# The last head pair of layer 4: recombined by two small matmuls in place of transfers

## The reference, cut to what matters

```
q = heads(_layernorm(x) @ Wq.T + bq)        # 16 heads of 16 channels
k, v = heads(ctx @ Wk.T + bk), heads(ctx @ Wv.T + bv)
w = softmax(q @ k.T / sqrt(16))             # 256 x 4096 for a head, 4 batches
out = merge(w @ v)                          # 256 tokens x 256 channels
x = x + out @ Wo.T + bo
```

## Time and profile before

| what | value |
|---|---|
| the three runs | 2039.83, 2045.66, 2051.41 us (median 2045.66) |
| the profiled execution | 2051.41 us, span 2051.5 us |
| busy in the span | PE 88%, DVE 74%, ACT 59%, POOL 11% |
| mean granted clock of TensorE | 0.943 of full |
| layer 4, pairs 0 to 31 | up to 1845.4 us in the span |
| its chain behind the last pair | 1845.4 to 1865.0 us |

### The profile page before, as it was taken

How to read it: one execution, slowest core, us unless ns; L and a number is a source line. 1 busy time by engine, 2 the same in 40 slices (tenths; PEclk the granted TensorE clock), 3 DMA queues, 4 the chain that set the end, 5 groups by cost and what they waited for, 6 DMA issues and landing times. The chain is left out here.

```text
span 2051.5 us, 32916 instructions
## 1 busy us (share of the span) xinstructions
PE 1795.8 (88%) x12549; PEld 1222.8 (60%) x12549; DVE 1518.3 (74%) x1768; ACT 1205.8 (59%) x2132; POOL 234.1 (11%) x243
## 2 busy tenths in 40 slices
PE   7989998878888885799998799999999999996754
PEld 5877785456655663678787455555555555554523
DVE  6546553469988995565655689999998999983565
ACT  1333332587667762443534188888887888892463
POOL 4223301000000000222322000010010000000000
PEclk8999998999999997899999899999999999998977
DMA  9798842147755662121213956557566646510000
GB/s 360 265 326 317 316 160 88 65 163 255 249 203 206 227 242 81 62 68 65 67 44 65 147 129 128 100 112 126 114 106 109 128 98 120 95 26 12 1 0 21
DMA packets 172012, 280.32 MB, mean 137 GB/s; under 512 B 21568, under 2 KB 100672, under 8 KB 164688
## 3 DMA queue, kind: packets, MB, share of 16 engines
q1 hardware_dynamic: 170128, 277.72, 48.2%
q10 hardware_dynamic: 1728, 0.49, 0.2%
HBM read 187.50 MB, written 88.15 MB: 134 GB/s over the span
## 5 line engine op out<-in xcount | busy, mean ns | idle before, releaser
L2193 DVE TENSOR_REDUCE xn_peaks<-psum 128x2 f32<-128x1024 f32 x512 | 621.4, 1224 | 42.7 <-PE psum L2019 34.9
L2148 ACT ACTIVATE moe_mix_transposed<-psum 128x512 f32<-128x512 f32 x1024 | 552.8, 597 | 71.9 <-PE psum L2024 20.7
L2024 PE MATMUL psum<-xn_q_stack,xn_k_words 50*128 50x256 f32 x2048 | 377.2, 307 | 12.8 <-DVE xn_peaks L2193 6.3
L2024 PEld LDWEIGHTS psum<-xn_q_stack,xn_k_words 50*128 50x128 f32 x2048 | 249.8, 186 | 214.5 <-ACT moe_mix_transposed L2148 185.9
L2019 PE MATMUL psum<-xn_k_words,xn_q_stack 50*128 50x512 f32 x1024 | 371.8, 450 | 5.9 <-DMA xn_q_stack<-q_rows 3.8
L2056 PE MATMUL psum<-moe_mix_transposed,xn_v 128*32 128x256 f32 x4096 | 328.8, 393 | 2.0 <-issue 0.3
L2019 PEld LDWEIGHTS psum<-xn_k_words,xn_q_stack 50*128 50x128 f32 x1024 | 185.4, 185 | 14.2 <-DVE xn_peaks L2193 7.4
L1133 DVE TENSOR_TENSOR_SCAN mx_state<-mx_decay,mx_state 128x1024 f32<-128x1024 f32 x64 | 151.5, 2367 | 4.2 <-POOL mx_decay L858 4.2
L321 PE MATMUL psum<-xw_ctx_natural,xw_weights_transposed 128*128 128x256 f32 x512 | 124.8, 389 | 13.3 <-DVE xw_weights_transposed L473 13.1
L2056 PEld LDWEIGHTS psum<-moe_mix_transposed,xn_v 128*32 128x32 f32 x4096 | 81.8, 108 | 73.7 <-issue 8.3
L723 ACT ACTIVATE ctx_k_words<-psum,ctx_bk 128x512 fp32r<-128x512 f32 x128 | 86.6, 684 | 57.0 <-PE psum L153 35.2
(11 more groups left out here) (318 smaller groups left out, 2576.2 us busy)
## 6 DMA issues: line engine op xcount, KB each, us to landing
xn_k_words<-k_words SPq DMA_DIRECT2D x384, 128.0 KB, 6.7
ctx_words<-xw_ctx_transposed_words SPq DMA_DIRECT2D x64, 512.0 KB, 7.1
ctx_chunk_words<-ctx_words SPq DMA_DIRECT2D x64, 512.0 KB, 5.4
k_words<-ctx_k_words SPq DMA_DIRECT2D x128, 256.0 KB, 2.4
v_all<-ctx_v SPq DMA_DIRECT2D x32, 544.0 KB, 3.1
xn_v<-v_all SPq DMA_DIRECT2D x32, 544.0 KB, 4.9
xw_mask<-in_mask_BxSxS_ik SPq DMA_DIRECT2D x8, 2048.0 KB, 7.7
xw_ctx_natural<-in_ctx SPq DMA_DIRECT2D x32, 512.0 KB, 6.4
```

Source lines behind the costliest of these rows:

```text
L2024: return pe.matmul(PS[:, narrow_bank("exp", n, step, a), half * S:(half + 1) * S], K[n % XN_KSLOTS][narrow_rows(a), kt * P:(kt + 1) * P], ...
L2148: act.activation(t["weights"][:, step % 4, a, :, :], bank.rearrange("p (t s) -> p t s", t=2), ACT.Exp, scale=XN_SCALE).then_inc(s.taken, 1)
L2193: dve.tensor_reduce(t["peaks"][:, m % 2, q, :, c], PS[:, 2 * (x % 2):2 * (x % 2) + 2, :], AX.X, ALU.max).then_inc(s.top_read, 1)
```

## The change

For the last pair (n = 31) alone, transfers and reciprocals go another way; pairs 0 to 30 are computed as before.

- A constant tile `choice` (2 matrices of 128x32, zeros and ones) is made by two small POOL instructions near the layer's start. The first matrix adds the two halves of a head's 16 rows, the second adds the two denominators and repeats them over 16 rows.
- `head_rows` is left out for n = 31. `spread_inverses(3)`, `halves(3)`, `inverted(3)` and `normalised(3)` treat the 7 other pairs of batch 3 (224 of 256 channels: all of channel block c = 0 and rows 0 to 95 of c = 1). SP reaches `spread_inverses(3)` behind `head_rows(30)`. On DVE they stand behind the same three `ffn_weight_dve` as before.
- PE, behind the last weighted sum: `last_projected(0)` (2 matmuls with channels 0 to 127, behind `s.o`), `chosen` (2 matmuls, 32 rows by 256 columns, from `sums` of the last pair into bank 2, behind `s.acc`), `last_projected(1)` (2 matmuls with channels 128 to 255, behind `s.last_o`). Each query tile has a bank of its own.
- DVE, behind `chosen`: the reciprocal of 32x256 denominators from PSUM, a product of 32x256, and then for both query tiles x plus the product straight from PSUM, and the statistics. ACT's copy to `proj` is gone.

```diff
+XN_END = XN_W * (P // XN_W - 1)
+XN_CHOSEN = 2
+def narrow_moved(b):
+    return XN_PAIRS - (b == B - 1)
+def narrow_parts(b):
+    return (0, P), (1, P if b < B - 1 else XN_END)
...
 def narrow_sp
     def spread_inverses(b):
+        there = 2 * narrow_moved(b)
         sp.wait_ge(s.den, 2 * (b + 1))
-        sp.dma_start(Rd[b]..., t["den"][:, 0, :]).then_inc(s.r_out, 16)
+        sp.dma_start(Rd[b, 0:there]..., t["den"][0:there * XN_SPREAD, 0, :]).then_inc(s.r_out, 16)
         sp.wait_ge(s.r_out, 16 * (b + 1))
         for c in range(KD):
-            heads = Rd[b, c * P // XN_DH:(c + 1) * P // XN_DH]
+            heads = Rd[b, c * P // XN_DH:min((c + 1) * P // XN_DH, there)]
...
     for n in range(XN_N):
-        head_rows(n)
+        if n < XN_N - 1:
+            head_rows(n)
...
-        if n % XN_PAIRS == XN_PAIRS - 1:
+        if n % XN_PAIRS == narrow_moved(n // XN_PAIRS) - 1:
             spread_inverses(n // XN_PAIRS)
...
 def narrow_pool
     def halves(b):
-        pool.wait_ge(s.o_in, 64 * XN_PAIRS * (b + 1))
+        pool.wait_ge(s.o_in, 64 * (XN_PAIRS * b + narrow_moved(b)))
...
+        for c, rows in narrow_parts(b):
+            last = pool.tensor_tensor(t["OT"][0:rows, c, :], t["O"][0:rows, c, 0, :], t["O"][0:rows, c, 1, :], ALU.add)
+        last.then_inc(s.halves, 1)
+    def choice():
+        ident = k.ident[:].rearrange("p (h a w) -> p h a w", h=2, a=2)
+        pool.tensor_tensor(t["choice"][:, 0, :, :], ident[:, 0, :, 0:XN_DH], ident[:, 1, :, 0:XN_DH], ALU.add
+                           ).then_inc(s.choice, 1)
+        ones = [ident[:, h, :, XN_DH:XN_VW].to_broadcast([P, 2, XN_DH]) for h in range(2)]
+        pool.tensor_tensor(t["choice"][:, 1, :, :], ones[0], ones[1], ALU.add).then_inc(s.choice, 1)
...
     query(2)
+    choice()
...
 def narrow_pe
+    def last_projected(c):
+        if c == 0:
+            pe.wait_ge(s.o, B)
+        else:
+            pe.wait_ge(s.last_o, 1)
+        for q in range(QT):
+            last = pe.matmul(PS[:, q, 0:D], t["OT"][:, c, q * P:(q + 1) * P], t["wo"][:, c, :], start=(c == 0),
+                             stop=(c == KD - 1))
+            if c:
+                last.then_inc(s.last_pe, 1)
+    def chosen():
+        pe.wait_ge(s.choice, 2)
+        pe.wait_ge(s.acc, XN_N)
+        for i in range(2):
+            last = pe.matmul(PS[XN_END:, XN_CHOSEN, i * S:(i + 1) * S], t["choice"][:, i, :, :]...,
+                             t["sums"][:, (XN_N - 1) % 2, :], start=True, stop=True)
+        last.then_inc(s.chosen, 1)
...
-    for kind, which in XN_LAST:
-        between[kind](which)
+    pe.wait_ge(s.top_read, XN_N * XN_TOP)
+    last_projected(0)
+    chosen()
+    last_projected(1)
...
 def narrow_act
     accumulated(XN_N - 1)
-    for kind, which in XN_LAST:
-        between[kind](which)
...
 def narrow_dve
     inverted(B - 1)
     normalised(B - 1)
-    projected(B - 1)
+    inverse = t["rsum"][XN_END:, KD - 1, :]
+    dve.wait_ge(s.chosen, 1)
+    dve.reciprocal(inverse, PS[XN_END:, XN_CHOSEN, S:2 * S]).then_inc(s.last_den, 1)
+    dve.wait_ge(s.last_den, 1)
+    dve.tensor_tensor(t["OT"][XN_END:, KD - 1, :], PS[XN_END:, XN_CHOSEN, 0:S], inverse, ALU.mult).then_inc(s.last_o, 1)
+    dve.wait_ge(s.plus, NT)
+    for q in range(QT):
+        i = (B - 1) * QT + q
+        dve.wait_ge(s.last_pe, q + 1)
+        dve.tensor_tensor(k.X[:, i, :], k.X[:, i, :], PS[:, q, 0:D], ALU.add).then_inc(s.x, 1)
+        dve.wait_ge(s.x, B + q)
+        dve.bn_stats(k.stats[:, i, :], k.X[:, i, :]).then_inc(k.ln.stats, 1)
```

More of the change, by code:

```diff
@@ L1675, in narrow_numbers @@
             uses += narrow_before(n, step) + [("exp", n, step, a) for a in range(2)]
-    XN_USE.update((use, r) for r, use in enumerate(uses + XN_LAST))
+    XN_USE.update((use, r) for r, use in enumerate(uses))
 narrow_numbers()
@@ L1727, in narrow_tiles @@
          "neg": sb("neg_max", [P, 2, QT * 2]), "neg_words": sb("neg_words", [P, QT, 2, XN_HALF], F32R),
-         "ident": sb("identity_words", [P, P], F32R), "sums": sb("sums", [P, 2, S]),
+         "choice": sb("choice", [P, 2, 2, XN_DH]), "ident": sb("identity_words", [P, P], F32R), "sums": sb("sums", [P, 2, S]),
          "den": sb("denominators", [P, 2, S // XN_SPREAD]), "rsum": sb("rsum_by_channels", [P, KD, S])}
@@ L1741, in narrow_sems @@
     s = k.sems("xn", "mix_pe mix_r mixed stats aggr root rstd y wq k_ones weights pads zeros made taken qlo q_out q_in top top_read "
-                     "neg words sum acc o_in den_in r_out r_in halves den ident o wide row plus x")
+                     "neg words sum acc o_in den_in r_out r_in halves den ident o wide row plus x "
+                     "choice chosen last_den last_o last_pe")
     return s, [k.xn_keys_in] + [k.sem_row(f"xn_keys{slot}_", XN_KHALVES) for slot in range(1, XN_KSLOTS)], k.sem_row("xn_values", 2)
@@ L1801, in spread_inverses @@
     def spread_inverses(b):
+        there = 2 * narrow_moved(b)
         sp.wait_ge(s.den, 2 * (b + 1))
-        sp.dma_start(Rd[b].rearrange("h (e s) -> (h e) s", e=XN_SPREAD), t["den"][:, 0, :]).then_inc(s.r_out, 16)
+        sp.dma_start(Rd[b, 0:there].rearrange("h (e s) -> (h e) s", e=XN_SPREAD), t["den"][0:there * XN_SPREAD, 0, :]
+                     ).then_inc(s.r_out, 16)
         sp.wait_ge(s.r_out, 16 * (b + 1))
         for c in range(KD):
-            heads = Rd[b, c * P // XN_DH:(c + 1) * P // XN_DH]
-            sp.dma_start(t["rsum"][:, c, :], heads[:, None, :].to_broadcast([P // XN_DH, XN_DH, S])).then_inc(s.r_in, 16)
+            heads = Rd[b, c * P // XN_DH:min((c + 1) * P // XN_DH, there)]
+            n = heads.shape[0]
+            sp.dma_start(t["rsum"][0:n * XN_DH, c, :], heads[:, None, :].to_broadcast([n, XN_DH, S])).then_inc(s.r_in, 16)
     for tile in t["K"]:
@@ L1884, in halves @@
     def halves(b):
-        pool.wait_ge(s.o_in, 64 * XN_PAIRS * (b + 1))
+        pool.wait_ge(s.o_in, 64 * (XN_PAIRS * b + narrow_moved(b)))
         if b:
             pool.wait_ge(s.made, XN_USE["projected", b - 1] + 1)
-        pool.tensor_tensor(t["OT"], t["O"][:, :, 0, :], t["O"][:, :, 1, :], ALU.add).then_inc(s.halves, 1)
+        if b < B - 1:
+            pool.tensor_tensor(t["OT"], t["O"][:, :, 0, :], t["O"][:, :, 1, :], ALU.add).then_inc(s.halves, 1)
+            return
+        for c, rows in narrow_parts(b):
[7 more added lines that the diff above has]
+        pool.tensor_tensor(t["choice"][:, 1, :, :], ones[0], ones[1], ALU.add).then_inc(s.choice, 1)
     pool.memset(t["V"][:, :, XN_KT * 2 * XN_VW:], 0.0).then_inc(s.pads, 1)
@@ L2091, in narrow_pe @@
                 weighted(n - 1, XN_STEPS + step - 2)
+    def last_projected(c):
[12 more added lines that the diff above has]
+        for i in range(2):
+            last = pe.matmul(PS[XN_END:, XN_CHOSEN, i * S:(i + 1) * S], t["choice"][:, i, :, :].rearrange("p a n -> p (a n)"),
+                             t["sums"][:, (XN_N - 1) % 2, :], start=True, stop=True)
+        last.then_inc(s.chosen, 1)
     for step in (XN_STEPS - 2, XN_STEPS - 1):
         weighted(XN_N - 1, step)
-    for kind, which in XN_LAST:
-        between[kind](which)
+    pe.wait_ge(s.top_read, XN_N * XN_TOP)
+    last_projected(0)
+    chosen()
+    last_projected(1)
 def narrow_act(k, t, sems):
@@ L2203, in inverted @@
     def inverted(b):
-        dve.wait_ge(s.den_in, 64 * XN_PAIRS * (b + 1))
-        dve.tensor_tensor(t["den"][:, 0, :], t["den"][:, 0, :], t["den"][:, 1, :], ALU.add).then_inc(s.den, 1)
+        den = t["den"][0:2 * narrow_moved(b) * XN_SPREAD, :, :]
+        dve.wait_ge(s.den_in, 64 * (XN_PAIRS * b + narrow_moved(b)))
+        dve.tensor_tensor(den[:, 0, :], den[:, 0, :], den[:, 1, :], ALU.add).then_inc(s.den, 1)
         dve.wait_ge(s.den, 2 * b + 1)
-        dve.reciprocal(t["den"][:, 0, :], t["den"][:, 0, :]).then_inc(s.den, 1)
+        dve.reciprocal(den[:, 0, :], den[:, 0, :]).then_inc(s.den, 1)
     def normalised(b):
@@ L2212, in normalised @@
         dve.wait_ge(s.halves, b + 1)
-        dve.tensor_tensor(t["OT"], t["OT"], t["rsum"][:], ALU.mult).then_inc(s.o, 1)
+        if b < B - 1:
+            dve.tensor_tensor(t["OT"], t["OT"], t["rsum"][:], ALU.mult).then_inc(s.o, 1)
+            return
+        for c, rows in narrow_parts(b):
+            last = dve.tensor_tensor(t["OT"][0:rows, c, :], t["OT"][0:rows, c, :], t["rsum"][0:rows, c, :], ALU.mult)
+        last.then_inc(s.o, 1)
     def projected(b):
```

1 line of the change is left out of this document (removed).

## The result

The changed kernel took 2042.25 us (median of 20 runs, 2033.84 to 2051.80) and the kernel before 2051.17 (median of 20, 2039.83 to 2065.50): ratio 0.9961, 95% interval 0.9942 to 0.9980. So it is faster by 0.39%, some 8 us, and less than the 10.5 forecast; in the prediction's terms it lies within 0.5%. (The two medians differ by 8.9.) The kernel before is 5.5 us slower by 20 runs than by the three from which I started (2045.66), so that the absolute time is off by 7.0 us, of which 5.5 is the starting point.

What follows compares the result with a forecast made beforehand. The prediction took a plain 19.65 us chain at layer 4's end as the bound; its rebuilt tail moved the barrier's end from 1865.03 to 1854.56, gaining 10.47 us. So 2045.66 - 10.5 = 2035.2 us, range 2028.3 to 2041.9.

Steps and rivals of the forecast that it cites:

- within 0.5%: Whole kernel's time: outcome class of no change that a measurement can tell, about 10.2 us; chance 0.46.
- In this time the clock is still full ... so 1.99: PE's eight records of the projection's first half and recombination in the tail: full clock, 1.99 us, ending at 1849.51.
- My own upper end, +1.8: The same eight PE records at the half clock: 3.75 us instead of 1.99.
- the range of 9.5 to 11.5: Main forecast for the whole kernel: 9.5 to 11.5 us gained; chance 0.72.
- the same holds here: Other seven pairs' transfers, from the store's issue to the start of `normalised`: 4.77 us as in the old tail.
- this rival: Transfers still set the end: 9.39 us against 4.77, PE starts 4.6 later, gain 5.9; chance 0.06.
- The hold by POOL: DVE's 48-column weight instruction held by POOL's `halves`: 0.3 us taken, 0 to 0.8 possible.
- The line through 32 and 48 columns: DVE's reciprocal of 32x256 from PSUM: 353 ns for 32 columns, 452 for 48, hence 1.74 us.
- I leave equal (0): PE's clock in the layer behind the barrier: unchanged; 0.7 gained if it stays full, up to 1.5 lost if later.
- The slow rival: Low clock through the next layer's dense block: change loses from 10.5 us on, 2077 us with all; chance 0.03.
- The one with the clock: PE's clock falls early, last matmul at half clock, and rises 1.5 dearer: gain 8.3, 2037.4 us; chance 0.11.
- the next thing to be late: `chosen` on PE, input ready at 1845.82, queued behind `last_projected(0)`, which waits for transfers until 1847.37.

Runs made afterwards that it cites:

- the late inversion: Changed kernel and versions keeping the other pairs' denominator reciprocals behind the third weight matrix; store issued 3.3 to 3.9 us ahead of the last weighted sum's end.
- both orders turned: Changed kernel with denominators inverted ahead of the third weight matrix and last pair recombined before the projection's first half; tail 6.72 us, ratio 0.9952 to the kernel before.

## Why the forecast gain was too high

The mechanism was right, the short chain in place of the long one; the gain in the tail was 6.96 and not 10.47. The missing 3.5 by the prediction's own terms:

- *"In this time the clock is still full ... so 1.99"*: this step failed, by 1.73. I took the fall near 1850, 4.6 us after PE had stopped, as the least time and let it cover a wait of 2.1 us. The wait was 3.9, because the transfers and the hold made the seven pairs late, and the clock fell. With idle matmuls the eight records took 2.06, in one execution of the changed kernel 2.1 by themselves. One profile was also too few for a least time. In the other five of the kernel before, the clock fell 1.9, 2.1, 2.3, 3.2 and 5.0 us after PE had stopped. So even the wait of 2.1 would not always have been covered. My own upper end, +1.8, was the value, and the range of 9.5 to 11.5 leaves it out.
- *"the same holds here"* for the 4.77 from the store's issue to the normalisation: 6.30, +1.53. It was 5.6 to 6.5 in six profiles with the late inversion, without added transfers, and with nothing else on DVE ahead of the normalisation; 0.5 to 1.2 of the excess is the store. Shape, pause and the work of PE and ACT are ruled out, and all nine slow stores lie on a code packet. It could be read beforehand: in the kernel before the packet starts at 1841.92, and the prediction put the store at 1841.86. I looked only at transfers that SP issues. The rest of the excess, 0.69 here and 0.2 to 0.7 in the six, is the load, whose cause is open. I let this rival stand as 4.6 or nothing, and not in between.
- *The hold by POOL*, taken as 0.3, measured 0.53 to 0.56, +0.26. The row of 0.87 was to be believed: DVE's instruction started as POOL's second one did and ended with it. The Trainium skill (SBUF — State Buffer, Who interferes with whom) says the same of a tensor_scalar in its two-port form, and the experiment with POOL's sums moved agrees, 0.19.
- Everything else held within 0.2: the first of the last two products took 0.16 more, reciprocal 1.76 (1.74), product 0.43 (0.42), x and statistics 1.67 (1.70), `normalised` 0.76 (0.74), barrier 0.31 (0.32). The line through 32 and 48 columns carried to 256 in PSUM. The Trainium skill's description of the divide (VectorE: DVE Perf Modes, First, the fixed hardware budget) gives 2.3 as an estimate; the measured 1.76 decides.
- *"I leave equal (0)"* for the part behind the barrier: the profiled pair differs by 6.4, all of it PE's clock. By the runs the loss must be smaller: 8.0 measured, 19.7 - 12.0 = 7.7 by the means of six tails of the kernel before and three of the changed one. If the high values belong to the change, the expected loss is about 3 (mean of eleven profiles less mean of six), and the gain left, some 4.7, is still inside the interval of the ratio (4.1 to 11.9 us).
- The range was built on three executions. Twenty put the kernel before at 2051.17, and the time, 2042.25, fell 0.35 above the range. A gain of the measured ratio from the 2045.66 would have been inside it.

The slow rival didn't come. The one with the clock came in part: the gain of 8.0 is near its 8.3, but it had priced only the last matmul at the half clock and not the eight records; it had 0.11. What I called "the next thing to be late", the recombination queued behind a half of the projection that waits for transfers, was indeed the place: with both orders turned, the tail is 6.7.

## What to carry to other kernels

When a chain is taken off the end of a layer, ask where the work that replaces it stands in each engine's own list: here the reciprocals stood behind a weight preparation on DVE that made them 6 us later than need be, and moving one call was worth 4.8 us of tail against the mean of the changed kernel's three, 5.5 against the first. Look for code packets too when you place a small transfer that others wait for. Give PE's work behind a wait of 2 us or more the half clock as a case of its own, unless something keeps PE busy; and where only the tail changed, compare tails, since the rest of the span varies by more than the gain.

## What was not expected of the hardware

- The clock's fall is not fixed: where PE had nothing to do behind the last weighted sum, it came 1.7 to 5.0 us after that in twelve profiles, and not within 3.17 us in one. Behind PE waits of 3.0 to 3.9 us it was at half for all or most of the eight records that followed in seven profiles, and full in one with 3.17.
- The stretch behind the barrier is a constant plus PE's busy time: 62.44 and 62.43 in the two profiles shown, and 62.4 to 62.5 in all seventeen without idle matmuls behind the barrier. Its spread of 186.5 to 193.2 is PE's clock alone.
- Matmuls whose results nobody reads can give back clock: 9 to 16 us of PE's busy time at the low clock became 4.4, and the stretch behind the barrier 182.60 us instead of 186.5 to 193.2.
- The same small store to device memory took 1.39 to 1.44 us until the next issue in nine profiles and 1.84 to 2.63 in nine others. In these one of its 16 landings came late, 1.05 to 1.09 us behind the end of a code packet of 16 KB that took 0.93 to 1.38.
